# Second attention of a fused two-layer block: banks of their own for the first two batches, a later recurrence, and the ternary weights prepared in the first attention

## The reference, cut to what matters

```
decay = exp(-exp(w)) * (0.5 + 0.5*tf);  ek = exp(min(k,30));  ekv = ek*v
n, d  = forward scan + backward scan of ekv and ek with that decay
euk   = exp(min(u + k, 30))
gate  = (n - ekv + euk*v) / (d - ek + euk)
_bi_wkv(r) = sigmoid(r) * gate * (0.8 + 0.2*tf)
x = x + attention0(_bi_wkv(x))     # queries, keys, values from one weight; softmax over rows and over columns
x = x + ffn0(_bi_wkv(x))           # fp8, one scale per tensor
x = x + attention1(_bi_wkv(x))     # w_q, w_k, w_v, w_o; rotary; causal
x = x + ffn1(_bi_wkv(x))           # w1, w2 made ternary: clip(round(w / mean|w|), -1, 1); int8 per token; relu squared
```

## Time and profile before

| | |
|---|---|
| time, median of 3 runs | 409.94 us (406.87 to 409.94) |
| profiled execution | 412.68 us, of which its span 410.9 us |
| busy, share of the span | PE 272.2 us (66%), DVE 296.3 (72%), ACT 208.4 (51%), POOL 40.4 (10%) |
| mean granted clock of PE | 0.784 of full speed |

### The profile page before, as it was taken

One profiled execution on the slowest core, in us unless ns is written; L12 is line 12 of the kernel. 1 busy time (PEld: TensorE's weight loads), 2 busy tenths in 40 slices (PEclk: granted clock), 3 DMA queues, 4 the chain that ended last, 5 costly groups with the idle time before them and its releaser, 6 DMA issues.

```text
span 410.9 us, 5220 instructions
## 1 busy us (share of the span) xinstructions
PE 272.2 (66%) x1867; PEld 154.9 (38%) x1867; DVE 296.3 (72%) x536; ACT 208.4 (51%) x422; POOL 40.4 (10%) x61
## 2 busy tenths in 40 slices
PE   0142746448539767756766687979897997976745
PEld 0122413224314324424331335536464553633633
DVE  3998999999797995776398969694657337055761
ACT  5715695866874956171342136434466344232631
POOL 4110120200210114001000101010000000000000
PEclk9999757857856757895685689698699698595996
DMA  6200225346244252004123523565000000000001
GB/s 225 69 0 1 53 51 102 72 77 161 53 77 78 51 104 52 0 2 83 21 45 57 104 51 57 98 186 122 0 2 2 0 2 0 2 0 2 26 26 53
DMA packets 8089, 22.22 MB, mean 54 GB/s; under 512 B 1536, under 2 KB 2944, under 8 KB 7680
## 3 DMA queue, kind: packets, MB, share of 16 engines
q0 software_dynamic: 4032, 14.68, 19.0%
q1 hardware_dynamic: 4032, 7.21, 5.3%
HBM read 6.16 MB, written 1.05 MB: 18 GB/s over the span
## 4 chain that ended last, share of the span: by engine, by line
DVE 37%; PE 33%; issue 12%; ACT 11%; DMA 5%; POOL 0%; DVEq 0%; ACTq 0%; POOLq 0%
DVE fwd L656 5%; PE PM L1105 5%; PE PS L1222 4%; ACT E L498 3%; PE PS L1112 3%; PE PM L1053 3%; DVE kp L885 3%; DMA fwd<-bwd 3%; PE PO L1238 3%; PE PM L1166 2%; DMA fwd<-mid 2%; PE PM L1175 2%; DVE bwd L662 2%; PE PS L1284 2%; DVE rsum L759 2%
## 5 line engine op out<-in xcount | busy, mean ns | idle before, releaser
L885 DVE TENSOR_REDUCE kp<-PS 128x2 f32<-128x256 f32 x64 | 32.3, 549 | 17.8 <-PE PS L1199 17.7
L576 ACT ACTIVATE E<-PS 128x384 f32<-128x384 f32 x64 | 27.8, 488 | 29.8 <-PE PS L1222 29.8
L1112 PE MATMUL PS<-identb 128*128 128x512 bf16 x86 | 31.3, 452 | 16.2 <-ACT E L576 8.7
L498 ACT ACTIVATE E<-PS,negc,escale 128x256 f32<-128x256 f32 x64 | 35.2, 567 | 6.9 <-PE PS L1067 6.9
L1080 PE MATMUL PO<-E,vt 128*32 128x256 f32 x256 | 25.8, 540 | 13.0 <-DVE ytok L787 9.5
L1053 PE MATMUL PM<-ident,kp 128*128 128x128 f32 x128 | 24.4, 353 | 12.8 <-DVE kp L702 7.3
L1088 PE MATMUL PO<-ident,yc 128*128 128x128 f32 x64 | 17.4, 364 | 20.0 <-ACT yc L473 19.9
L490 ACT ACTIVATE E<-PS,negc,escale 128x1024 f32<-128x1024 f32 x16 | 19.2, 1200 | 20.2 <-PE PS L1067 20.2
L1067 PE MATMUL PS<-TP 32*128 32x256 f16 x256 | 21.3, 344 | 8.5 <-DVE TP L714 6.1
L1053 PEld LDWEIGHTS PM<-ident,kp 128*128 128x128 f32 x128 | 19.4, 182 | 18.1 <-issue 9.3
L307 POOL DMA_DIRECT2D fwd<-mid x14 | 12.2, 871 | 132.4 <-DVE fwd L656 132.4
(11 more groups left out here) (179 smaller groups left out, 616.7 us busy)
## 6 DMA issues: line engine op xcount, KB each, us to landing
fwd<-mid POOLq DMA_DIRECT2D x14, 512.0 KB, 4.5
fwd<-bwd POOLq DMA_DIRECT2D x14, 512.0 KB, 4.5
kT<-in_kT SPq DMA_DIRECT2D x4, 256.0 KB, 4.3
xT<-in_xT SPq DMA_DIRECT2D x4, 256.0 KB, 6.2
G<-in_attn SPq DMA_DIRECT2D x1, 1024.0 KB, 4.9
ek<-in_w SPq DMA_DIRECT2D x1, 1024.0 KB, 5.2
ekv<-in_w SPq DMA_DIRECT2D x1, 1024.0 KB, 9.4
out<-mid SPq DMA_DIRECT2D x8, 128.0 KB, 1.7
```

Source lines behind the costliest of these rows:

```text
L498: nc.scalar.activation(E[:, p % 4, i, v * T:(v + 1) * T], PS[:, 2 + i, v * T:(v + 1) * T], ACT.Exp, bias=negc[:], scale=escale[:], accum_o ...
L576: nc.scalar.activation(E[:, p % 4, i, 0:384], PS[:, i, 0:384], ACT.Exp, scale=QSCALE).then_inc(S["e1_done"], 1)
L885: nc.vector.tensor_reduce(kp[:, b % 2, u * H + 2 * j:u * H + 2 * j + 2, D], PS[:, at0:at0 + 2, lo:hi], AX, ALU.max, negate=True).then_inc( ...
L1112: nc.tensor.matmul(bank, identb[:], identb[:, None, :].broadcast_to([P, 4, P]), start=True, stop=True)
```

## The change

1. **Banks.** Values of batches 0 and 1 go to a bank of PO, which the first attention has left; queries of batch 0 are transposed into PS banks 0 and 1, its keys into PS banks 2 and 3. Waits that kept PM apart go. `project_qk`, values, queries and keys of the first two batches move to slots -16, -16, -15, -15 and -14, -14, -9, -9 (before: -16, -15, -14, -13 and -12, -11, -10, -9). Six idle matmuls are added.
2. **Recurrence.** Steps 10 to 15 get a table of six slots each. Step 10's `inputs` and `ahead` now stand after the first `rotary`. `gated(2, 2)` and `gated(2, 3)` go from slots -3 and 5 to -2 and 7.
3. **Rings.** `mid` and `bwd` are used as rings of two: `prepare(n)` waits for the DMA of step n - 2 (before: n - 3), and `behind(n)` gets a wait for the second DMA of step n - 2. The third parts hold the ternary weights.
4. **Weights.** SP loads `w1` and `w2` at the start, into `G[3]` and `halfs`. In the first attention ACT sums absolute values (slots 0 and 4), scales and rounds (12 and 20) and takes the rounding constant off (16 and 24); PE adds over partitions in slot 9, DVE scales in slot 10. DVE clamps in one operation each in slots 6 and 8 of the second attention.

```diff
-        WKV1 = {-18: 10, -12: 11, -6: 12, -2: 13, 2: 14, 5: 15}
+        GATED2 = (None, None, -2, 7)
+        STEP1 = {10: (-17, -15, -15, -13, -4, -3),
+                 11: (-4, -2, 0, 1, 5, 6),
+                 12: (4, 6, 7, 8, 13, 14),
+                 13: (8, 10, 11, 12, 17, 18),
+                 14: (13, 14, 15, 16, 21, 22),
+                 15: (17, 18, 19, 20, 25, 26)}
+        PREPARE1, INPUTS1, AHEAD1, BEHIND1, LN1, GATE1 = range(6)
...
+        WEIGHT_ABS = (0, 4)
+        WEIGHT_SUM = 9
+        WEIGHT_ROUND = (12, 20)
+        WEIGHT_INT = (16, 24)
+        CLAMP = (6, 8)
-        AT_QK = (-16, -12, 0, 8)
-        AT_V = (-15, -11, 1, 9)
-        AT_Q = (-14, -10, 2, 10)
-        AT_K = (-13, -9, 3, 11)
+        AT_QK = (-16, -14, 0, 8)
+        AT_V = (-16, -14, 1, 9)
+        AT_Q = (-15, -9, 2, 10)
+        AT_K = (-15, -9, 3, 11)
...
+        def v_bank(b):
+            return PO[:, 0, :] if b < 2 else PM[:, 0, :]
+
+        def q_banks(b):
+            return PS[:, 0:2] if b == 0 else PM[:]
+
+        def k_banks(b):
+            return PS[:, 2:4] if b == 0 else PM[:]
...
+            sp.dma_start(w1f, w1_d).then_inc(S["ld_w1"], 16)
+            sp.dma_start(w2f, w2_d).then_inc(S["ld_w2"], 16)
             sp.wait_ge(S["a_done"], B)
             sp.dma_start(w1a, attn1_d).then_inc(S["ld_attn1"], 16)
-            sp.wait_ge(S["scan_done"], 4 * LAYERS * B)
-            sp.wait_ge(S["m_done"], LAYERS * B)
-            sp.dma_start(w1f, w1_d).then_inc(S["ld_w1"], 16)
-            sp.dma_start(w2f, w2_d).then_inc(S["ld_w2"], 16)
...
+            def weight_abs(n):
+                act.wait_ge(S[f"ld_w{n + 1}"], 16)
+                nc.scalar.activation(G[2][:, :], (w1f, w2f)[n], ACT.Abs,
+                                     accum_out=wsc[:, n:n + 1]).then_inc(S["wabs_done"], 1)
+            def weight_int(n):
+                act.wait_ge(S["wround_done"], n + 1)
+                nc.scalar.activation((w1q, w2q)[n], (w1f, w2f)[n], ACT.Copy, bias=-ROUND).then_inc(S["wint_done"], 1)
...
+                if n >= 2 + EARLY:
+                    dve.wait_ge(S[f"back_added{(n - 2) % RING}"], added(n - 2))
...
-                link(nc.vector.tensor_scalar(q, w, -ROUND, 1.0, ALU.add, ALU.min))
-                nc.vector.tensor_scalar(q, q, -1.0, None, ALU.max).then_inc(S["wq_done"], 1)
+                nc.vector.tensor_scalar(q, q, 1.0, -1.0, ALU.min, ALU.max).then_inc(S["wq_done"], 1)
...
                 if b == 1:
-                    pe.wait_ge(S["kT1_done"], 1)
+                    pe.wait_ge(S["rope_done"], TT)
...
             def project_v(b):
-                pe.wait_ge(S["rope_done"], TT * b + 1)
+                if b == 1:
+                    pe.wait_ge(S["v1_done"], 1)
+                if b >= 2:
+                    pe.wait_ge(S["rope_done"], TT * b + 1)
...
                 for bb in due(AT_Q, p):
-                    turn(bb, 0, "qtr_done", [("qkp_done", 2 * TT * (bb + 1)), ("padq_done", bb + 1), ("v1_done", bb + 1)])
+                    if bb == 0:
+                        heat(PO[:, 1, :], 3)
+                        pe.wait_ge(S["y8_done"], B)
+                    turn(bb, 0, "qtr_done", [("qkp_done", 2 * TT * (bb + 1)), ("padq_done", bb + 1)]
+                         + ([("v1_done", bb + 1)] if bb >= 2 else []), q_banks(bb))
                 for bb in due(AT_K, p):
-                    turn(bb, TT * H, "ktr_done", [("qTb_done", bb + 1)])
+                    turn(bb, TT * H, "ktr_done", [("qTb_done", bb + 1)] if bb else [], k_banks(bb))
+                    if bb == 0:
+                        heat(PO[:, 1, :], 3)
```

More of the change, by code:

```diff
@@ L480, in _ @@
                 b, j = divmod(p, PAIRS)
+                for n in due(WEIGHT_ABS, p):
+                    weight_abs(n)
+                for n in due(WEIGHT_ROUND, p):
+                    weight_round(n)
+                for n in due(WEIGHT_INT, p):
+                    weight_int(n)
                 for n in steps0(p, 6):
@@ L520, in _ @@
             tanh(2, B - 1)
-            prepare(min(WKV1.values()))
+            prepare(min(STEP1))
             nc.scalar.preload_act_table_set("natural_log_exp_and_others")
-            def weight_round(n):
-                act.wait_ge(S["wscale_done"], 1)
-                w = (w1f, w2f)[n]
-                nc.scalar.activation(w, w, ACT.Copy, scale=wsc[:, 4 + n:5 + n],
-                                     bias=ROUND).then_inc(S["wround_done"], 1)
             def hqT_copy(t):
@@ L556, in _ @@
                     yT_copy(bb, "ytr1_done", "out1_done", "yT1_done")
[L557 removed]
+                for n in steps1(p, LN1):
                     wkv(n)
[L559 to L561 removed]
+                for n in steps1(p, PREPARE1):
+                    prepare(n)
                 for bb in due(RESIDUAL1, p):
@@ L983, in final @@
                                                ALU.mult, ALU.add).then_inc(S["res_done"], 1)
-            inputs(10)
-            for i in range(2):
-                ahead(10, i)
             for p in SLOTS1:
@@ L1022, in _ @@
                     heads_out(p // 2 - 3)
-                if p in (18, 20):
-                    weight_ternary((p - 18) // 2)
-                for n in steps1(p, 7):
+                for n in due(CLAMP, p):
+                    weight_ternary(n)
+                for n in steps1(p, GATE1):
                     gate(n)
-                wkv(steps1, p)
+                for n in steps1(p, INPUTS1):
+                    inputs(n)
+                for n in steps1(p, AHEAD1):
+                    for i in range(2):
+                        ahead(n, i)
+                for n in steps1(p, BEHIND1):
+                    for i in range(2):
+                        behind(n, i)
         @block.tensor
@@ L1043, in project0, with turn @@
                 ins.then_inc(S["proj0_done"], 1)
-            def turn(b, first, done, wait):
+            def turn(b, first, done, wait, into=PM):
                 for s, n in wait:
@@ L1120, in _ @@
                     scores0(p)
+                if p == WEIGHT_SUM:
+                    pe.wait_ge(S["wabs_done"], 2)
+                    pe.wait_ge(S["pads_set"], 4)
+                    pe.wait_ge(S["qT0_done"], 2 * (b + 1))
+                    if b >= 2:
+                        pe.wait_ge(S["x_done"], b - 1)
+                    nc.tensor.matmul(PM[:, 1, 0:2], ones[:], wsc[:, 0:2], start=True, stop=True)\
+                        .then_inc(S["wsum_done"], 1)
                 if p % 2 == 1 and 0 <= (p - 5) // 2 < B * CH:
```

137 lines of the change are left out of this document (61 added, 76 removed).

## The result

| kernel | median | runs | profiled execution | its span | mean granted clock |
|---|---|---|---|---|---|
| before | 409.8 us | 4, 406.9 to 409.9 | 412.7 us | 410.9 us | 0.784 |
| after | 396.7 us | 4, 395.3 to 398.7 | 398.7 us | 396.9 us | 0.784 |

The ratio is 0.970 with a 95% interval of 0.964 to 0.976. The profiled pair differs by 14.0 us, the medians by 13.1. The forecast was 19.2 us of the profiled execution, 391 us. The profiled execution of the kernel before counts as a slow one of that kernel, 0.7% above its median, so a difference of two profiles in which it takes part can be larger than that of the medians.

The account below looks back on a forecast made before the run. DVE bounds the first attention, single-step chains the second's start, DVE the stretch to slot 0, then PE. Front gain 22.5 less 3.3 lost in slots 0 to 31 gives 19.2 us off 412.7: 393.5, median 391; forecast 386 to 397, full range 383 to 401.

Parts of the forecast that it names:

- The start and the way to slot 0: Start of the second attention gains 13 us; first row maximum to slot 0 gains 8.5 us.
- The front's term: Everything up to slot 0 and the hoped-for faster project_qk(2): gain 22.5 us, bounds 19 and 25.
- The microsecond hoped for at `project_qk(2)`: This projection may run at 3.70 instead of 5.69 us: gain 0 to 2 us, taken as 1.
- the 13 us that I gave to the new start: Start of the second attention: earlier rotary and projection bring the first row maximum 12.8 us forward.
- Weights in the first attention at 0: Six ACT passes, 12 us, covered by holes in the first attention: cost 0, bounds 0 and loss 6.
- tail at 0: From slot 32 on nothing changes but buffers: 0.
- The step that was mis-sized: slots 16 to 25: Slots 16 to 20 sum to 0; slot 20 loses 1.3 us and slot 25 loses 1.6.
- a loss of 3.3 us: Slots 0 to 31, where moved recurrence work arrives: loss 3.3 us, bounds gain 2 and loss 9.
- Rival 4: Slots 0 to 31: denser PE work keeps more at the lower clock; slower, about 418 us; chance 0.04.
- The gain of the weights in slots 12 to 20: Sums, roundings and ternary operations leave: gain 0.5 us in slots 10 to 15, 0 in slots 16 to 20.
- Rival 2: Three weight passes and all four added table loads are exposed: 8.5 us less gain, 400 us; chance 0.14.
- Rival 3: Slots 0 to 20: moved scans and inputs hold up maxima; 14 of 17 us return, 405 to 407; chance 0.07.

Follow-up runs that it names:

- e7: Changed kernel with the old banks, slots and waits for values, queries and keys; recurrence and weights as changed: 398.4 us, ratio 0.976.
- e8: Kernel before with the weights alone moved (early load, ACT's six passes in the first attention, one clamp each): 400.1 us, ratio 0.980.
- e4: Changed kernel with steps 11 to 15 of the recurrence in about their old slots; banks and weights as changed: 390.1 us, ratio 0.956.
- e1: Changed kernel with a plain copy instead of Ln for steps 13 to 15 (computation changed): 393.8 us, ratio 0.966.
- e11: Changed kernel with the eight scans of steps 14 and 15 over 8 columns instead of 512 (computation changed): 395.2 us, ratio 0.970.
- e5: Changed kernel with behind(10) moved from slot -13 to -9, behind the first three row maxima: 393.6 us, ratio 0.962.

## Why the prediction was right on the whole, and 5 us too good

**The start and the way to slot 0: right.** First maximum 193.3 (predicted 194.9), slot 0 at 212.4 (212.3), the second projection 3.60 us at the higher level as chosen. The front's term was 22.5; the exponentials of slot 0 are 22.1 earlier. That slot 0 fits to 0.1 us is luck: the rotary began 1.4 us earlier than I had it, for which the forecast has no term, and DVE's hole was 5.25 us, not 3, since the two turns ran at the lower level. The microsecond hoped for at `project_qk(2)` did not come (5.71 us). The price of such a projection at the lower clock was read wrongly as well: in the 5.83 us at 198.41 the granted clock is 0.50 for the first part only and 0.62 in the mean, so at the lower level throughout it would be longer. The split between causes that my account suggests doesn't hold, though: e7 has slot 0 as early without the banks, so in this kernel the order of the recurrence makes the front's gain, and the 13 us that I gave to the new start were not the banks' alone. With the old order, the banks and step 10's place are worth 9.8 us at slot 0 (e8 to e4).

**Weights in the first attention at 0, tail at 0: right.** ACT has 10 us more there (I had 12), and slot 0 of e8 is 1.1 us late.

**The step that was mis-sized: slots 16 to 25.** For slots 0 to 31 I had a loss of 3.3 us; it was 8.0 (from 22.1 to 14.1), within its bound of 9. Of this, slots 16 to 20 were priced at 0 and lost 7.7; slots 20 to 24 at 1.3 and gained 2.9; slots 24 to 27 at 1.6 and lost 4.8. Three things in that term were wrong, and slots 24 to 27 are the two loads, as e1 shows.
- I had one table load ahead of each Ln. There are two, one for Ln and one for the Exp behind it. "ScalarE: Activation LUTs" of the Trainium skill, section "Table sets: the hidden batching unit", counts one load for Ln followed by Exp. Here L435 and L437 have three each, and the measurement decides. Six were added in place of four, and none for the tanh of slots 24 and 31. The 1.38 us of drain that the same page adds to a load (section "What ACT_TABLE_LOAD costs") is not in the rows: the load at 284.37 ends at 285.65, and Ln starts at 285.67.
- I went through DVE's queue for what delays maxima, and not for what delays the residual of slot 16. `ahead(14)`'s two scans stand before it, and its tanh and the exponentials of slot 16 wait for it. With the scans short, PE's wait there fell from 1.92 to 0.64 us (e11).
- I priced each delay at its own length. In slots 24 to 27 two loads of 2.57 us cost 4.8. Slot 16's wait of 1.92 us was followed by 17 us at 1.2 GHz. Rival 4 has the clock, but over all of the slots and from denser work (its 418 us are 420 by its own terms); here it fell in one place, after a wait, and the mean of the stretch stayed (0.82 against 0.83), since slots 0 to 16 were at 0.90 where before they had 0.85.

**The gain of the weights in slots 12 to 20: far under-sized.** I gave 0.5 us for the two sums and let the rest be absorbed. e8 gives 8 us for the weights alone. In the profiles most of it goes with the clock: slots 13 to 14 at 1.00 instead of 0.55, slots 14 to 22 at 1.00 instead of 0.88. That moving the sums and passes keeps the clock up is argued and not shown.

**Rivals.** Rival 2 was right on the table loads in slots 24 to 27, and wrong on the weights. Rival 3, the moved work comes back, is wrong by its number (405 to 407), and right as a mechanism: measured against e4, the later recurrence gains 13.4 us by slot 0 and has lost it all, and 5.9 more, at slot 31. Of these 19.3 us, 11.4 are in slots 14 to 22, and 4.9 in slots 24 to 27, which are table loads and not scans. The total hid this, since the weights and banks gained more than I had for them. So that the sum came near was in part luck: two terms were wrong in opposite directions. By ratios, of 410 us:

```
weights alone                                   8 us less      (e8)
banks and step 10's new place, on top          10 us less      (e8 to e4)
later recurrence, on top of both                6 us more      (e4 to after)
later recurrence without the banks              2 us less, not resolved (e8 to e7)
```

**What stays open.** How the loss between slots 14 and 22 divides between table loads, scans, `prepare` and the clock: in the whole time, taking the loads and Ln gave 3 us, the scans 1.5, putting the Ln together 1.7, naming the set nothing, each near the scatter of this kernel's medians. The runs differ from after by single parts of the schedule, and no run takes loads and scans away together while all else keeps its slot.

What the lower level costs is shown by rows of the same work at both levels. What makes the clock fall is shown for slots 24 to 27: two loads of ACT taken away, PE's wait is 0.39 us instead of 3.19, and the fall doesn't come (e1). There is no rule in it for other places. The falls at 195 and 284 us follow waits of 2.51 and 1.92 us, and e5's wait of 3.07 us up to 207.40 was followed by a fall within two microseconds (0.50 from 209 to 211). But after's wait of 1.81 us up to 306.72 was followed by none, and the kernel before fell at 292 us behind a wait of 1.13 that e8 has too, without a fall. So the length of the last wait isn't the whole rule.

Nor does the mean granted clock of an execution order its time: the changed kernel took 398.7, 396.8, 395.3 and 396.6 us at 0.784, 0.853, 0.792 and 0.862. A single profiled execution of this kernel carries its own falls, so differences of 1 us between two of them mean nothing. Why e4's front gains only 8.8 us although its banks are the new ones wasn't tried further.

## What to carry to other kernels

Judge a change of several parts by its parts: here one part of three cost 6 us, and the total looked like a success. In a chain where PE takes turns with two in-order queues, a few microseconds of other work ahead of the one op that PE waits for can cost more than their length (in slots 24 to 27, 2.57 us of loads cost 4.8), so look for the slot whose residual, tanh or copy they delay and not only for the maxima. When Ln moves in among tanh, count the table sets, and when an op that reads a DMA's sum moves earlier, count that DMA's landing.
